# Normed x loaded transposed from the host instead of turned on TensorE, in a cross-attention and feed-forward kernel

## The reference

```
x = x + xattn(layernorm(x), ctx, ctx)      # q = layernorm(x), k = v = ctx
    pre = [q,k,v] @ ifgate_w.T + ifgate_b;  pre = 15*tanh(pre/15)
    log_d = cumulated log sigmoid(f) + i, causal;  m = max over keys
    h = ((q k^T)/sqrt(32) * exp(log_d - m)) v / (max(|row sum|, exp(-m)) + 5e-5)
    h = h * rsqrt(mean(h*h) + 1e-6) * (1 + outnorm_w)      # 8 heads of 32
x = x + ffn(layernorm(x))
    h = silu(x W1 s1) * (x W2 s2);  h = gelu(h H1 s3);  h = gelu(h H2 s4);  return h W3 s5
```

## Time and profile before

| | us |
|---|---|
| median of 3 runs | 764.75 (764.41 to 764.94) |
| the profiled execution | 764.41 |
| its span in the trace | 762.7 |
| PE busy | 754.7 (99%) |
| DVE busy | 543.6 (71%) |
| ACT busy | 384.1 (50%) |
| POOL busy | 53.7 (7%) |
| granted TensorE clock, share of full speed | 0.999 |

### The profile page before, as it was taken

The page is one execution under the profiler, slowest core; times in us unless marked ns, Lnnn a source line. Parts: engine busy times, 40 slices in busy tenths (PEclk is TensorE's granted clock), DMA queues, the critical chain, the costliest instruction groups (busy, mean ns, idle before and its releaser), DMA issues.

```text
span 762.7 us, 15214 instructions
## 1 busy us (share of the span) xinstructions
PE 754.7 (99%) x6296; PEld 631.7 (83%) x6296; DVE 543.6 (71%) x1295; ACT 384.1 (50%) x577; POOL 53.7 (7%) x67
## 2 busy tenths in 40 slices
PE   8999999999999999999999999999999999999998
PEld 4778888888898888988888888888889888898887
DVE  6788786696957868588676877658695784965554
ACT  3566456463365634556454554646335562445332
POOL 3400020000100020000200002000020000000000
PEclk9999999999999999999999999999999999999999
DMA  9393112200022000310005001230102100540640
GB/s 327 98 426 110 35 52 88 108 29 30 29 112 83 29 31 28 140 56 29 31 29 193 0 31 39 87 127 23 37 29 112 55 1 3 172 160 11 177 144 30
DMA packets 14617, 63.46 MB, mean 83 GB/s; under 512 B 2016, under 2 KB 2896, under 8 KB 11728
## 3 DMA queue, kind: packets, MB, share of 16 engines
q1 hardware_dynamic: 12960, 50.12, 18.9%
q0 software_dynamic: 1296, 11.53, 3.9%
q10 hardware_dynamic: 288, 0.79, 0.3%
HBM read 53.94 MB, written 8.50 MB: 82 GB/s over the span
## 4 chain that ended last, share of the span: by engine, by line
PE 94%; DVE 1%; ACT 0%; issue 0%
PE ps_f L1601 31%; PE ps_f L1602 30%; PE ps_f L1566 8%; PE ps_f L1567 8%; PE ps_f L1641 4%; PE ps_f L1642 4%; PE ps_a L1506 2%; PE ps_a L1489 2%; PE ps_a L1341 1%; PE ps_a L1539 1%; PE ps_a L1462 1%; PE ps_a L1455 1%; PE ps_a L1498 0%; PE ps_f L1576 0%; DVE stats L1063 0%; DVE z L1050 0%
## 5 line engine op out<-in xcount | busy, mean ns | idle before, releaser
L1601 PE MATMUL ps_f<-h_hi,wgt 128*128 128x512 f32 x1024 | 401.5, 392 | 0.0
L1602 PE MATMUL ps_f<-h_lo,wgt 128*128 128x512 f32 x1024 | 398.7, 389 | 0.0
L1601 PEld LDWEIGHTS ps_f<-h_hi,wgt 128*128 128x128 f32 x1024 | 192.2, 188 | 40.5
L1602 PEld LDWEIGHTS ps_f<-h_lo,wgt 128*128 128x128 f32 x1024 | 192.3, 188 | 39.0
L752 ACT ACTIVATE work<-ps_f,scl 128x512 f32<-128x512 f32 x128 | 87.5, 684 | 164.9 <-PE ps_f L1602 164.3
L1169 DVE TENSOR_TENSOR h_lo<-work,h_hi 128x512 fp32r<-128x512 f32 x128 | 86.6, 690 | 101.7 <-ACT h_hi L757 100.6
L1566 PE MATMUL ps_f<-h_hi,wgt 128*128 128x512 f32 x252 | 99.1, 393 | 0.0
L1567 PE MATMUL ps_f<-h_lo,wgt 128*128 128x512 f32 x252 | 98.3, 390 | 0.0
L739 ACT ACTIVATE work<-ps_f,scl 128x512 f32<-128x512 f32 x64 | 44.2, 690 | 88.2 <-PE ps_f L1567 87.5
L757 ACT ACTIVATE h_hi<-work 128x512 fp32r<-128x512 f32 x128 | 81.0, 633 | 4.1
L1160 DVE SCALAR_TENSOR_TENSOR work<-ps_f,scl,work 128x512 f32<-128x512 f32 x64 | 48.1, 751 | 39.4 <-PE ps_f L1567 37.9
(11 more groups left out here) (214 smaller groups left out, 685.2 us busy)
## 6 DMA issues: line engine op xcount, KB each, us to landing
decay<-m_rows SPq DMA_DIRECT2D x14, 1024.0 KB, 6.6
decay<-w_cols SPq DMA_DIRECT2D x22, 512.0 KB, 4.2
wgt<-w_cols POOLq DMA_DIRECT2D x5, 1024.0 KB, 11.8
v_aug<-ctx_tok SPq DMA_DIRECT2D x8, 528.0 KB, 3.9
wgt<-w_cols POOLq DMA_DIRECT2D x2, 2048.0 KB, 14.1
x_kept<-xs SPq DMA_DIRECT2D x8, 512.0 KB, 2.6
xs<-x SPq DMA_DIRECT2D x7, 512.0 KB, 3.6
ctxT<-ctx_t SPq DMA_DIRECT2D x7, 512.0 KB, 3.3
```

The costliest lines, as they stand in the source:

```text
L1601: pe.matmul(ps_f[:, bank], w, moving(h_hi[layer][:, k], as_is), start=(k == 0), stop=False)
L1602: last = pe.matmul(ps_f[:, bank], w, moving(h_lo[layer][:, k], as_is), start=False, stop=(k == KH - 1))
```

## The change

The host passes a second copy of x, transposed, and from pair 2 on this copy is loaded straight into zT. The mean and the root of each token still come from z on DVE, but are then kept in a small tile, written to DRAM, and read back to all 128 partitions over the tile z, where the raw x is no longer needed. POOL subtracts the mean from zT, DVE multiplies by the root, and ACT rounds zT from SBUF. PE's turn of z goes from the passes, and so do DVE's four L901 and ACT's L616.

```
-def build(nc, x, ctx_tok, ctx_t, gate_w, gate_b, outnorm_w, w_cols, scales, w3_s, out):
+def build(nc, x, x_t, ctx_tok, ctx_t, gate_w, gate_b, outnorm_w, w_cols, scales, w3_s, out):
...
         x1_kept = nc.dram_tensor("x1_kept", [PAIRS, P, Q, DIM], F32, kind="Internal").ap()
         m_rows = nc.dram_tensor("m_rows", [BH, SEQ], F32, kind="Internal").ap()
+        moment_rows = nc.dram_tensor("moment_rows", [2, P, Q], F32, kind="Internal").ap()
         wgt = sb("wgt", [P, COLS], F32R)
         h_hi = [sb(f"h_hi{n}", [P, KH, NT], F32R) for n in range(2)]
...
+        moments = sb("moments", [P, 2, Q])
...
+        s_moments = sem("s_moments")
+        s_moments_out = sem("s_moments_out")
+        s_moments_in = sem("s_moments_in")
+        s_xT = sem("s_xT")
+        s_xT_centred = sem("s_xT_centred")
...
         def ctxT(j):
             return work[:, CH:2 * CH] if first(j) else ctxT_buf[:]
+        def moment_spread(k):
+            per_token = z[:].rearrange("p q d -> p (q d)").rearrange("p (k t q) -> p k q t", k=2, q=Q)[:, k]
+            return per_token.rearrange("p (o q) t -> p o q t", o=1).to_broadcast([P, CH, Q, P])
+        def by_tile(a):
+            return a.rearrange("p c (q t) -> p c q t", q=Q)
         def plain(j):
             return j < W
...
         @block.sync
         def _(sp):
             def load_z(j):
-                sp.wait_ge(s_zT, j)
+                if j > W:
+                    sp.wait_ge(s_zTe, j)
+                else:
+                    sp.wait_ge(s_zT, j)
                 sp.dma_start(z[:], x[j]).then_inc(s_zin, 16)
+            def spread_moments(j):
+                sp.wait_ge(s_moments, j - W + 1)
+                reuse(sp, s_moments_in, 16 * (j - W))
+                sp.dma_start(moment_rows.rearrange("k p q -> p k q"), moments[:]).then_inc(s_moments_out, 16)
+                sp.wait_ge(s_moments_out, 16 * (j - W) + 16)
+                sp.dma_start(z[:].rearrange("p q d -> p (q d)"),
+                             moment_rows.rearrange("(o k) p q -> o (k p q)", o=1).to_broadcast([P, 2 * NT])).then_inc(s_moments_in, 16)
+            def load_xT(j):
+                sp.wait_ge(s_farmm, j)
+                sp.dma_start(zT(j), x_t[j]).then_inc(s_xT, 16)
             def load_ctxT(j):
                 reuse(sp, s_qk, W * j if j > 1 else 0)
...
                 if g < PAIRS:
                     load_z(g)
                     load_ctxT(g)
+                    spread_moments(g)
+                    load_xT(g)
                     load_v(g)
                 if j < PAIRS:
                     keep_x1(j)
...
                 pool.wait_ge(s_keys_hi, j - W + 1)
                 pool.tensor_tensor(keys_lo, ctxT(j), keys_hi.bitcast(F32), ALU.subtract).then_inc(s_keys_lo, 1)
+            def centre(j):
+                pool.wait_ge(s_moments_in, 16 * (j - W) + 16)
+                pool.wait_ge(s_xT, 16 * (j - W) + 16)
+                pool.tensor_tensor(by_tile(zT(j)), by_tile(zT(j)), moment_spread(0), ALU.subtract).then_inc(s_xT_centred, 1)
             def split_normed_low(j):
                 pool.wait_ge(s_zhi, j - W + 1)
                 pool.tensor_tensor(normed_lo, zT(j), normed_hi.bitcast(F32), ALU.subtract).then_inc(s_zlo, 1)
...
                 if j < PAIRS:
                     weigh_keys(j)
                 if g < PAIRS:
+                    centre(g)
                     split_keys_low(g)
                     split_normed_low(g)
...
                     act.wait_ge(s_zT, 1)
                     act.activation(zT(j)[:, 1], source[:, 1], ACT.Copy).then_inc(s_zTe, 1)
                     return
-                act.wait_ge(s_zT, j + 1)
-                act.activation(zT(j), source, ACT.Copy).then_inc(s_zTe, 1)
                 if plain(j):
+                    act.wait_ge(s_zT, j + 1)
+                    act.activation(zT(j), source, ACT.Copy).then_inc(s_zTe, 1)
                     return
+                act.wait_ge(s_zTe, j + 1)
                 reuse(act, s_gate, j)
                 if j >= 2:
                     act.wait_ge(s_mm, 2 * KH * (j - 2) + KH)
-                act.activation(normed_hi, source, ACT.Copy).then_inc(s_zhi, 1)
+                act.activation(normed_hi, zT(j), ACT.Copy).then_inc(s_zhi, 1)
             def take_gate_low(j):
                 act.wait_ge(s_gate, j + 1)
...
             def norm_1_apply(j):
                 if plain(j):
                     dve.wait_ge(s_zT, j)
-                norm_apply(j, xs[j] if plain(j) else z, z, s_z)
+                norm_apply(j, xs[j], z, s_z)
+            def keep_moments(j):
+                reuse(dve, s_moments_out, 16 * (j - W))
+                dve.tensor_copy(moments[:, 0], mv[:, :, 0])
+                dve.tensor_copy(moments[:, 1], nw[:, 3, 0:Q]).then_inc(s_moments, 1)
+            def scale_centred(j):
+                dve.wait_ge(s_xT_centred, j - W + 1)
+                dve.tensor_tensor(by_tile(zT(j)), by_tile(zT(j)), moment_spread(1), ALU.mult).then_inc(s_zTe, 1)
             def norm_2_stats(j, src):
                 norm_stats(s_norm2, j, src)
...
                         norm_1_stats(g)
                     if g_stage and m == 4:
                         norm_rsqrt(s_norm1, g)
-                        norm_1_apply(g)
+                        keep_moments(g)
                     if a_stage and m == 5:
                         take_state(j)
                     if a_stage and m == 6:
                         take_far(j)
                     if a_stage and m == 7:
                         take_num(j)
+                        if g_stage:
+                            scale_centred(g)
                         mix_divide(j)
                     if last:
                         compare(COMPARED_BEFORE_LAST + m)
...
                     pass
                 def between_3(k):
-                    if g_stage and k == 3:
-                        turn_z(g)
+                    pass
                 def within_3(m):
                     pass
...
     v_aug = np.ones((PAIRS, P, Q, HEADS, DV), np.float32)
     v_aug[..., 0:DH] = tok(ctx).reshape(PAIRS, P, Q, HEADS, DH)
     ctx_t = np.ascontiguousarray(ctx.reshape(PAIRS, NT, CH, P).transpose(0, 3, 2, 1))
+    x_t = np.ascontiguousarray(np.asarray(x).reshape(PAIRS, NT, CH, P).transpose(0, 3, 2, 1))
     def up(w):
...
-        "x": tok(x), "ctx_tok": v_aug, "ctx_t": ctx_t, "gate_w": gate_w, "gate_b": gate_b,
+        "x": tok(x), "x_t": x_t, "ctx_tok": v_aug, "ctx_t": ctx_t, "gate_w": gate_w, "gate_b": gate_b,
```

29 lines of the change are left out of this document (25 added, 4 removed).

## The result

| | before | after |
|---|---|---|
| median, us | 764.69 (6 runs, 764.41 to 765.35) | 789.07 (6 runs, 785.7 to 790.61) |
| the profiled execution, us | 764.41 | 788.99 |
| its span, us | 762.7 | 787.2 |
| PE busy, us | 754.7 | 759.3 |
| granted clock, mean | 0.999 | 0.989 |

The account below looks back on a forecast made before the run. PE, busy 754.7 of 762.7 us, was taken as the bound. DVE 3.4 us later, against 0.85 slack and with PE's turn 0.86 shorter, loses 2.55 per pass; six times, 15.3 on 764.41 is 779.7, said as 780; range 768 to 791.

Parts of the forecast that it names:

- The bound, and the slack of 0.85 us at the turn of the rows: PE is the limit; at the second hidden layer's end DVE's L962 is done 0.85 us before PE needs it.
- DVE rigid behind L1169: DVE busy 21.44 of 22.83 us after 279.09; a microsecond added there is a microsecond later at L962, in six passes.
- Two-operand work of POOL holds up DVE's: DVE instructions with two SBUF operands stand until POOL's ends: L1104 takes 2.04 us instead of 0.22; L1115 stands too.
- The rival in which it stays hidden: No hold-up of DVE at the new places, PE keeps its full 0.86 us per pass: 759.2 us, faster; chance 0.12.
- Sizes: POOL's centring 2.4 us, DVE's product 1.7 (1.22 to 2.15), L1169 ending at 281.3, L1113 at 287.5, L1115 at 290.1.
- the step from PE's wait to the time: PE's later start at the turn of rows, 2.55 us lost per pass, taken six times as 15.3 us.
- a PE idle of 2.8 us: Sign in the profile after: PE idle near 2.8 us before the turn of rows, released by L962, six times.
- The later order of the locks: x lands after 279.1, L1169 slips in, product precedes keys' low part: L1115 5.6 later, 793 us; 0.17 with late moments.

Follow-up runs that it names:

- the last version: The version with the early product, with the statistics of z, root and moments also moved earlier on DVE: 760.88 us, ratio 0.9945 to the kernel before.
- the run with eight fill products: The changed kernel with 8 identity products of 128 columns on PE, into an unread bank, ahead of the wait for the turn of rows: 782.07 us.
- the version with unit steps: The changed kernel with moments stored in DRAM tile by tile, so POOL and DVE read mean and root word by word without a step: 817.81 us.
- the one without the wait on POOL: The version with the early product, without the wait that keeps POOL's keys' low part back for the division: 765.06 us, ratio 1.0006.
- the version with the early product: The changed kernel with centring and product moved ahead of L1169 into DVE's idle time, context loaded later, POOL's low parts reordered: 765.54 us.

## Why the prediction was right, and which term was missing

- *The bound, and the slack of 0.85 us at the turn of the rows.* Right. PE's turn was worth 0.89 us (0.86 forecast), read where PE does not wait. DVE's slack, less the 0.05 us from the rows to their turn, is the 0.78 of the line, and the last version uses both up: PE just meets the rows.
- *DVE rigid behind L1169.* Right: the 3.4 us at L1115 were 3.4 us at L962, and in each experiment what L1115 lost came out again at the scan, to within 0.1 us (in some last passes 0.25).
- *Two-operand work of POOL holds up DVE's.* Right, at each of the places named, and in the order named. The rival in which it stays hidden (759.2) fell with the first row of the profile after.
- *Sizes.* The centring was 0.5 too short and the product 0.14; L1169, which had to wait for the rest of the centring, was 0.4 late. At L1113's end 0.3 us of this was left. It was made good behind that: POOL's last subtraction ended 2.25 us after L1113, where 2.4 was forecast, and L1115 0.05 us after that, where 0.2 was. The sum hit 290.1, and that it did so to a hundredth is luck. On the product the forecast weighed the Trainium skill (Vector Engine (DVE) Microarchitecture Reference, Measured stream behaviour on trn2), which by an estimate gave 1.85 to 2.6 us where I took 1.7; measured are 1.84 behind a stand and 1.97 to 2.02 without one. The Trainium skill was nearer.
- *What failed: the step from PE's wait to the time.* The forecast took "this is 2.55 us lost per pass" and multiplied it by six. It was 2.6 lost by waiting and, in five passes, 1.45 by the lower clock behind the stand. This term was missing, about 7 us by the run with eight fill products. With it the forecast would have been 787; the waiting, the larger term, was right. The prediction itself had named a PE idle of 2.8 us and did not ask what PE does behind one. Before the change there was no such stand in the steady passes and no row of a low clock there, so its size could not be read; that it may not be nothing could.
- *The later order of the locks.* In the last pass x landed so late that the centring began 0.3 us behind L1222:

```profile
570.79 3.17 POOL L589 TENSOR_TENSOR zT<-zT,z 128x1024 f32<-128x1024 f32 x1 [31.59 <-DMA zT<-x_t]
573.91 2.39 POOL L584 TENSOR_TENSOR h_lo<-ctxT,h_hi 128x1024 fp32r<-128x1024 f32 x1
```

```profile
573.99 4.16 DVE L969 TENSOR_TENSOR zT<-zT,z 128x1024 f32<-128x1024 f32 x1 [2.19 <-POOL zT L589]
```

  Half of the rival came: the low part slipped in. The other half, the product getting in ahead of the keys' low part, did not; L969 began 0.08 us behind it. L1115 ended 0.9 us later than in the other passes, not 2.2.

What is still open is why the clock fell behind some stands of PE and not behind others of the same length: not in the third pass here, not in three passes without the product, and in none of the three such passes of the version with unit steps. The fill shows that the lower clock goes when PE does not stand; the runs do not say when a stand brings it.

## What to carry to other kernels

Taking work from the busiest engine pays only up to the slack of the next one; here 0.9 us came off PE and 3.4 us went onto the chain that had 0.85 us to spare. The same new work costs nothing in DVE's idle time some microseconds earlier, so look for the place before judging the idea. And when a forecast contains a wait of PE of some microseconds, give the products behind it at the lower clock a term of their own, with a chance.

## What the runs showed of the hardware that was not expected

- A stand of PE of 2.4 us was followed by 1.2 GHz for about 3.4 us in five passes of six, at 1.45 us each. In the version without the product, stands of 2.6 to 3.0 us were followed by it in three of six; in the one without the centring, stands of 1.8 us in one of six; in the one without the wait on POOL, the one stand of 2.5 us was; in the one with unit steps, stands of 2.4 to 2.6 us ahead of the rows in none of three, but some stands of 1.7 to 3.5 us elsewhere were. Behind stands of up to 1.2 us ahead of the rows no trace shows it.
- A second operand with a step of four words cost POOL 0.53 us over 1024 columns (2.92 against 2.39) and DVE 0.76 us (1.84 against 1.08).
- Who goes next when DVE's and POOL's two-operand instructions meet: a DVE instruction already standing goes in when POOL's ends, ahead of one that POOL has queued (L1222 after). One that waits for POOL's result by a semaphore comes behind POOL's next (L969 in the last pass, and in all six passes of the version with unit steps).
- A store of 4 KB in 1024 pieces of one word delayed what waits for it by 9.0 to 11.6 us, against 1.6 to 2.7 us in pieces of four words, and the latter spread alone made the version with the early product 0.3 to 1.0 us late.
